# A chain of recurrent layers on one core: r, c and p products in two halves of 64 columns, and TensorE's loop over two steps

## Chip, cores and metric

The kernel runs on 1 core of one Trainium2 chip. The metric is the device time of one execution in microseconds. Times are given as in the trace; "4041.36" is a moment, in microseconds from the start of the profiled span.

## What is computed

Four layers follow each other on x of shape 2 x 2048 x 512 (batch B = 2, T = 2048 time steps, D = 512), each added to its input. `cond` is 2 x 512. All is fp32.

```python
x = x + rnn(x, cond)        # h = tanh(h @ Wh + x_t @ Wx + b), step by step
x = x + x * softmax(q . x / sqrt(D), over the 2 batch rows)
x = x + tanh(x @ W_ih.T + (cond @ W_hh.T + b_hh + b_ih))
x = x + gru(x, cond)

# gru, step by step:
z = sigmoid([x_t, h] @ Wz + bz);  r = sigmoid([x_t, h] @ Wr + br)
c = tanh([x_t, r * h] @ Wh + bh)
h_new = (1 - z) * h + z * c                     # the output of the step
h = tanh(h_new @ Wp + bp) if (t + 1) % 4 == 0 and t < T - 1 else h_new
```

Both recurrences go through all 2048 steps in order. Within a step of the gru, c needs r, and the next step's r and z need c. The step after every fourth one needs the propagation p as well.

## The kernel before

The time axis is cut into 128 chunks (CHUNKS) of 16 steps (STEPS); 16 steps x 2 batch rows are the 32 rows (ROWS) of one quadrant. The 512 features lie as 128 partitions x 4 tiles (KT). The layers run as a pipeline over iterations i = 0 to 129: in iteration i the rnn does chunk i, the middle layers do chunk i - 1, and the gru does chunk i - 2 (LAG = 2). What of x does not depend on the recurrence is projected for a whole chunk at a time (`project_rnn_input`, `project_mid`, `project_gates`), goes through DRAM and comes back as "seeds": ScalarE copies the row of a step into a PSUM bank (L659), and TensorE adds the product with the state to it.

TensorE runs one list of products. A step's products are r, z, c, l in this order (`group`): r and z of the gru from the state, c from rh = r * h, and l, the rnn's step. Each of the four has the state (128 partitions x 2 columns) as its stationary operand and 128 columns of weights as its moving one. `seeded_product` (L398) issues 4 tiles k x 4 quadrants j of them:

```python
for k in range(KT):
    if ready is not None and k in (0, FRONT):
        pe.wait_ge(ready[k // FRONT], count)
    for j in range(NJ):
        last = nc.tensor.matmul(psum[QUAD * j:QUAD * j + B, 0:P], stationary(k), w[:, k, P * j:P * (j + 1)], ...)
```

The chip runs an fp32 matmul in two passes, so the trace shows x32 for a product of 16 matmuls. The four quadrants j write to four groups of partitions.

After r's product VectorE transposes the bank in two pieces (L539), k = 0 (32 columns, "front") and k = 1 to 3 (96 columns, "others"); ScalarE takes tanh of each piece (L714); VectorE makes rh of each piece (L602); TensorE's c product waits for the front piece at k = 0 and for the others at k = 1. From c to the new state it is the same: transposes of the pieces (L539), tanh (L724), the scan (L647) that writes `h_ring`, and TensorE's next r. TensorE has other work meanwhile: z between r and c, l between c and the next r. After the fourth step of a group (PROP = 4) stand the product p, and one projection of the middle layers: the input of the third layer (`project_mid`) in group q = 0, halves of the gates' input (`project_gates`, 384 columns) in q = 1 and 2, the rnn's input (`project_rnn_input`) in q = 3. Then r of the next group needs tanh of p (L734).

The softmax's logits (L434, 32 columns) come after step 2 of a chunk. GpSimd does the middle layers' elementwise work, and adds the gru's output to x3 once for four steps (`outputs`, L319).

TensorE's code is unrolled in iterations 0 to 2 and 126 to 129. Between them is a loop over i (L504), in it one over the four groups q (L505) whose body holds four steps (r, z, c, l four times), with branches that choose the logits (L507) and the projection (L511, L512, L517). Register and branch instructions are in the same queue as the matmuls. The q loop ends with adding to q, a compare-and-branch back, and one register instruction at its head (FUSED_REGOPS) that works out the counts of the step; at the end of i also the i loop's, two moves and a branch.

Of the kernel before, what the change touches and what calls it, by code (L numbers as in the profile page):

```python
# [34 lines left out]
B, T, D = 2, 2048, 512  # L35
P = 128
QUAD = 32
# [5 lines left out]
PROP = 4  # L43
# [3 lines left out]
FRONT = 1  # L47


def cond_resid_kernel(nc, xT, condT, w_rnn_x, w_rnn_h, b_rnn, w_ih, w_hh, b_ih, b_hh,  # L50
# [5 lines left out]
    with ctx:  # L56
# [6 lines left out]
        def piece_sems(name):  # L63
            return [sem(name + "_front"), sem(name + "_others")]
# [53 lines left out]
        l_ring = sb("l_ring", PROP, KT, B)  # L118
# [4 lines left out]
        h_prop = sb("h_prop", KT, B)  # L123
# [4 lines left out]
        h_ring = sb("h_ring", PROP, KT, B, 2)  # L128

        def bank(name):  # L130
            return ctx.enter_context(nc.psum_tensor(name, [P, 512], fp32))
        ps_r, ps_z, ps_c, ps_l, ps_p, ps_logit, ps_mid, ps_proj = (
            bank(n) for n in ("ps_r", "ps_z", "ps_c", "ps_l", "ps_p", "ps_logit", "ps_mid", "ps_proj"))
# [4 lines left out]

        r_T, c_T, p_T = ([bank[:, P:2 * P].rearrange("p (k r) -> p k r", k=KT)[:, k, :] for bank, k in
                          ((front, slice(0, FRONT)), (others, slice(FRONT, KT)))]  # L140
                         for front, others in ((ps_p, ps_r), (ps_p, ps_c), (ps_r, ps_p)))
# [10 lines left out]
        r_seeded, r_product = sem("r_seeded"), sem("r_product")  # L152
        r_T_done, r_tanh_done = piece_sems("r_T_done"), piece_sems("r_tanh_done")
        z_seeded, z_product, z_T_done, z_tanh_done = (sem(n) for n in ("z_seeded", "z_product", "z_T_done", "z_tanh_done"))
        c_seeded, c_product = sem("c_seeded"), sem("c_product")
        c_T_done, c_tanh_done = piece_sems("c_T_done"), piece_sems("c_tanh_done")
        h_neg_half_done, z_done, kept_done = sem("h_neg_half_done"), sem("z_done"), sem("kept_done")
        rh_ready, h_ready = piece_sems("rh_ready"), piece_sems("h_ready")

        p_seeded, p_product = sem("p_seeded"), sem("p_product")  # L160
        p_T_done, p_ready = piece_sems("p_T_done"), piece_sems("p_ready")
# [32 lines left out]

        def rnn_behind(i, u):

            return not isinstance(i, int) or 0 < STEPS * i + u <= STEPS * CHUNKS
# [4 lines left out]

        def first_step(i, u):

            return isinstance(i, int) and i == LAG and u == 0
# [10 lines left out]

        PIECES = [(slice(0, FRONT), slice(0, QUAD * FRONT)), (slice(FRONT, KT), slice(QUAD * FRONT, P))]

# [3 lines left out]
        def _(sp):  # L222
# [43 lines left out]
            def iteration(i):  # L266
# [22 lines left out]
                if gru:  # L289
                    sp.wait_ge(y_ready, GROUPS * (i - LAG + 1))  # L290
                    sp.dma_start(out[i - LAG, :, :, :], y[:, :, :]).then_inc(stored, 16)
# [5 lines left out]
        def _(pool):  # L297
# [16 lines left out]
            def outputs(i, q):  # L314

                pool.wait_ge(h_ready[1], STEPS * (i - LAG) + PROP * (q + 1))
                rows = slice(PROP * B * q, PROP * B * (q + 1))
                for k in range(KT):
                    last = tt(y[:, k, rows].rearrange("p (t b) -> p t b", b=B), x3[:, k, rows].rearrange("p (t b) -> p t b", b=B),  # L319
                              h_ring[:, :, k, :, 1], ALU.add)  # L320
                last.then_inc(y_ready, 1)

            def iteration(i):
                rnn, mid, gru, proj = running(i)
                if mid:
# [15 lines left out]

                    pool.wait_ge(top_done, i)
# [5 lines left out]
                    tt(denom[:, :], epair[:, :, 0], epair[:, :, 1], ALU.add).then_inc(denom_done, 1)  # L348
                    pool.wait_ge(inv_done, i)
# [6 lines left out]
                if gru:  # L356
                    after(pool, stored, 16 * (i - LAG))
                    outputs(i, 0)
                if mid:
# [5 lines left out]
                    last.then_inc(mid_pre_done, 1)  # L365
                    pool.wait_ge(mid_tanh_done, i)
                    tt(x3_new[:, :, :], x2[:, :, :], mid_tanh[:, :, :], ALU.add).then_inc(x3_new_done, 1)
                if gru:
                    for q in range(1, GROUPS):
                        outputs(i, q)  # L370
                    pool.wait_ge(y_ready, GROUPS * (i - LAG + 1))
# [7 lines left out]
        def _(pe):  # L379
# [9 lines left out]
            def seeded_product(psum, stationary, w, ready, count):  # L389
# [4 lines left out]
                for k in range(KT):  # L394
                    if ready is not None and k in (0, FRONT):
                        pe.wait_ge(ready[k // FRONT], count)
# [3 lines left out]
                return last  # L400

# [19 lines left out]
            for psum in (ps_l, ps_z, ps_p, ps_r, ps_c):  # L421
                open_bank(psum).then_inc(banks_open, 1)
# [3 lines left out]
            pe.wait_ge(states_set, 2)  # L426
# [4 lines left out]
            def softmax_logits(i):  # L431
                pe.wait_ge(qx_sum_done, i)
                for j in range(NJ):
                    last = nc.tensor.matmul(ps_logit[QUAD * j:QUAD * (j + 1), 0:ROWS], ones[:, :], qx_sum[:, :], start=True, stop=True)  # L434
# [13 lines left out]
            def group(i, t_rnn, t_gru, q, logits, projection):  # L448

                rnn, mid, gru, proj = running(i)
                for u in range(PROP):
                    if gru:
                        if u == 0:
                            ready, count = (p_ready, t_gru) if not first_step(i, PROP * q) else (None, None)
                            state = lambda k: h_prop[:, k, :]
                        else:
                            ready, count = h_ready, t_gru + u
                            state = lambda k: h_ring[:, u - 1, k, :, 1]  # L460
                        if first_step(i, PROP * q + u):
                            pe.wait_ge(r_seeded, 1)
                            pe.wait_ge(c_seeded, 1)
                            pe.wait_ge(p_seeded, PROP)
# [323 lines left out]
```

## Time and profile before

| | |
|---|---|
| median of 3 runs | 8794.18 us |
| range of the runs | 8787.57 to 33782.32 us |
| the profiled execution | 8793.52 us |
| its span | 8791.7 us |
| granted TensorE clock | 0.997 of full |
| busy: TensorE, VectorE, ScalarE, GpSimd | 8661.0, 5044.1, 4687.6, 997.6 us |
| the chain that ended last | TensorE 98%, issue 1% |

A row of the timeline merges instructions of one kind that follow each other. Its length reaches to the modelled end of the last matmul, and consecutive rows of TensorE overlap by that, so the pace is read from the starts. "PEld" is the load of the stationary operand, and a bracket says how long the engine sat idle and what released it. "PEldq" rows are instructions that only TensorE's queue handles: branches and registers. "issue" is waiting that no semaphore explains.

### The profile page before, as it was taken

How to read it: one execution, taken by the hardware profiler on the slowest of the kernel's cores; microseconds unless marked ns; L12 is line 12 of the kernel's file. 1: busy time of each engine (PE TensorE's matmuls, PEld its weight loads, DVE VectorE, ACT ScalarE, POOL GpSimd, SP SyncE). 2: the span in 40 equal slices, each digit the busy share in tenths (PEclk: the TensorE clock that was granted, in tenths of full speed). 3: DMA queues.
4: the chain of work that ended last, by engine and by line, in shares of the span. 5: the costliest groups of instructions: out<-in, count | busy, mean ns of one | idle time of the engine just before them, and what ended most of it. 6: DMA issues, size and time to landing. Idle time of an engine off the chain costs nothing.

```text
span 8791.7 us, 669547 instructions
## 1 busy us (share of the span) xinstructions
PE 8661.0 (99%) x291880; PEld 6952.4 (79%) x291880; DVE 5044.1 (57%) x26506; ACT 4687.6 (53%) x26367; POOL 997.6 (11%) x4362
## 2 busy tenths in 40 slices
PE   8999999999999999999999999999999999999998
PEld 6778777877787778778787778777877787778776
DVE  3555555555555555555555555555555555555555
ACT  3555555555555555555555555555555555555554
POOL 1111111111111111111111111111111111111110
PEclk8999999999999999999999999999999999999999
DMA  1000000000000000000000000000000000000000
GB/s 67 11 12 10 10 11 12 10 10 10 13 10 10 10 13 10 10 10 12 11 10 10 11 12 10 10 11 12 10 10 10 13 10 10 10 13 10 10 11 11
DMA packets 133369, 105.97 MB, mean 12 GB/s; under 512 B 14976, under 2 KB 132096, under 8 KB 132096
## 3 DMA queue, kind: packets, MB, share of 16 engines
q1 hardware_dynamic: 133248, 104.20, 3.9%
q8 instruction: 95, 1.56, 0.1%
q14 instruction: 26, 0.21, 0.0%
HBM read 62.20 MB, written 41.94 MB: 12 GB/s over the span
## 4 chain that ended last, share of the span: by engine, by line
PE 98%; issue 1%; DVE 0%; ACT 0%; DMA 0%; SPq 0%; POOL 0%; DVEq 0%; ACTq 0%
PE ps_r L398 23%; PE ps_c L398 22%; PE ps_l L398 21%; PE ps_z L398 20%; PE ps_p L398 6%; PE ps_mid L385 5%; PE ps_proj L385 2%; DVE l_T L536 0%; DVE ps_p L539 0%; PE ps_logit L434 0%; DMA rnn_h<-w_rnn_h 0%; DVE h_ring L647 0%; ACT l_ring L685 0%; ACT ps_l L659 0%; ACT scan_add L724 0%
## 5 line engine op out<-in xcount | busy, mean ns | idle before, releaser
L398 PE MATMUL ps_l<-rnn_h,l_ring 128*2 128x128 f32 x65536 | 2179.3, 274 | 26.8 <-ACT ps_l L659 26.8
L398 PE MATMUL ps_c<-c_h,rh 128*2 128x128 f32 x65536 | 2165.0, 272 | 6.3 <-DVE rh L602 2.4
L398 PEld LDWEIGHTS ps_c<-c_h,rh 128*2 128x2 f32 x65536 | 1397.2, 84 | 543.8 <-DVE rh L602 376.3
L398 PEld LDWEIGHTS ps_l<-rnn_h,l_ring 128*2 128x2 f32 x65536 | 1723.8, 85 | 112.2 <-ACT ps_l L659 36.9
L398 PE MATMUL ps_r<-r_h,h_ring 128*2 128x128 f32 x49152 | 1671.7, 272 | 18.7 <-DVE h_ring L647 18.7
L398 PE MATMUL ps_z<-z_h,h_ring 128*2 128x128 f32 x49152 | 1623.8, 273 | 0.2 <-issue 0.2
L398 PEld LDWEIGHTS ps_r<-r_h,h_ring 128*2 128x2 f32 x49152 | 994.9, 83 | 542.4 <-DVE h_ring L647 478.9
L398 PEld LDWEIGHTS ps_z<-z_h,h_ring 128*2 128x2 f32 x49152 | 1291.6, 85 | 50.4 <-issue 0.6
L539 DVE STREAM_TRANSPOSE ps_p<-ps_r 128x32 f32<-128x32 f32 x2048 | 473.4, 231 | 1329.0 <-PE ps_r L398 1329.0
L539 DVE STREAM_TRANSPOSE ps_p<-ps_c 128x32 f32<-128x32 f32 x2048 | 473.6, 231 | 1128.3 <-PE ps_c L398 1128.3
L319 POOL TENSOR_TENSOR y<-x,h_ring 128x8 f32<-128x8 f32 x2048 | 347.6, 201 | 4951.9 <-DVE h_ring L647 4951.9
L718 ACT ACTIVATE z_tanh<-z_T 128x8 f32<-128x8 f32 x2048 | 428.6, 209 | 883.1 <-DVE z_T L536 883.0
L647 DVE TENSOR_TENSOR_SCAN h_ring<-scan_mul,scan_add 128x4 f32<-128x4 f32 (+1 forms) x4096 | 720.8, 178 | 160.6 <-ACT scan_add L724 0.4
L685 ACT ACTIVATE l_ring<-l_T 128x8 f32<-128x8 f32 x2048 | 429.4, 210 | 703.7 <-DVE l_T L536 703.7
L724 ACT ACTIVATE scan_add<-ps_p 128x2 f32<-128x2 f32 x2048 | 352.4, 172 | 838.3 <-DVE ps_p L539 838.3
L714 ACT ACTIVATE r_tanh<-ps_p 128x2 f32<-128x2 f32 x2048 | 352.5, 172 | 817.1 <-DVE ps_p L539 812.7
L602 DVE SCALAR_TENSOR_TENSOR rh<-r_tanh,h_neg_half 128x2 f32<-128x2 f32 (+1 forms) x4096 | 683.8, 169 | 165.2 <-ACT r_tanh L714 0.7
L536 DVE STREAM_TRANSPOSE z_T<-ps_z 128x128 f32<-128x128 f32 x2048 | 648.7, 317 | 131.4 <-PE ps_z L398 1.6
L536 DVE STREAM_TRANSPOSE l_T<-ps_l 128x128 f32<-128x128 f32 x2048 | 648.4, 317 | 67.9 <-PE ps_l L398 65.7
L398 PE MATMUL ps_r<-r_h,h_prop 128*2 128x128 f32 x16384 | 541.0, 272 | 58.6 <-issue 53.2
L398 PEld LDWEIGHTS ps_r<-r_h,h_prop 128*2 128x2 f32 x16384 | 406.1, 84 | 239.8 <-issue 140.8
L539 DVE STREAM_TRANSPOSE ps_c<-ps_c 128x96 f32<-128x96 f32 x2048 | 595.0, 291 | 0.0
(85 smaller groups left out, 9399.0 us busy)
## 6 DMA issues: line engine op xcount, KB each, us to landing
gates_spill<-gates_rows SPq DMA_DIRECT2D x128, 192.0 KB, 1.9
gates_seeds<-gates_spill SPq DMA_DIRECT2D x512, 48.0 KB
x_next<-xT SPq DMA_DIRECT2D x128, 64.0 KB, 1.7
x_mid<-xT SPq DMA_DIRECT2D x128, 64.0 KB, 1.7
rnn_spill<-rnn_rows SPq DMA_DIRECT2D x128, 64.0 KB, 1.5
rnn_seeds<-rnn_spill SPq DMA_DIRECT2D x512, 16.0 KB
y_out<-y SPq DMA_DIRECT2D x128, 64.0 KB, 1.6
rcz_x<-w_rc_x SPq DMA_DIRECT2D x1, 2048.0 KB, 9.0
```

Of the source, the lines that this page charges most:

```text
L319: last = tt(y[:, k, rows].rearrange("p (t b) -> p t b", b=B), x3[:, k, rows].rearrange("p (t b) -> p t b", b=B), h_ring[:, :, k, :, 1], AL ...
L385: last = nc.tensor.matmul(psum[QUAD * j:QUAD * j + rows, 0:width], stationary(k), weights(k, j), start=(k == 0), stop=(k == KT - 1))
L398: last = nc.tensor.matmul(psum[QUAD * j:QUAD * j + B, 0:P], stationary(k), w[:, k, P * j:P * (j + 1)], start=False, stop=(k == KT - 1), sk ...
L536: return nc.vector.transpose(tile, psum[:, 0:P])
L539: nc.vector.transpose(pieces[n].rearrange("p k r -> p (k r)"), psum[:, PIECES[n][1]]).then_inc(T_done[n], inc)
L602: nc.vector.scalar_tensor_tensor(rh[:, k, :], r_tanh[:, k, :], 1.0, h_neg_half[:, k, :], ALU.subtract, ALU.mult).then_inc(rh_ready[n], 1)
L647: nc.vector.tensor_tensor_scan(h_ring[:, u % PROP, k, :, :].rearrange("p k b s -> p (k b s)"), scan_mul[:, k, :, :].rearrange("p k b s -> ...
L685: nc.scalar.activation(l_ring[:, u % PROP, :, :], l_T[:, :, 0:B], ACT.Tanh).then_inc(l_ready, 1)
L714: nc.scalar.activation(r_tanh[:, k, :], r_T[n][:, :, 0:B], ACT.Tanh, scale=-0.5).then_inc(r_tanh_done[n], 1)
L718: nc.scalar.activation(z_tanh[:, :, :], z_T[:, :, 0:B], ACT.Tanh, scale=0.5).then_inc(z_tanh_done, 1)
L724: nc.scalar.activation(scan_add[:, k, :, 0], c_T[n][:, :, 0:B], ACT.Tanh).then_inc(c_tanh_done[n], 1)
```

## The change

- r and c are computed in two halves of 64 columns (n = 0, 1; W = 64). Half n of all quadrants goes to a bank of its own: `ps_r` and `ps_c` are now two banks each. p shares the banks of c at other columns, and the logits share the bank of `ps_proj`. The order of the 8 parts (k, n), each of 4 matmuls, is: (0,0), (0,1), (1,0) once the low piece of the state is there, then, after the wait for the high piece, the rest of n = 0, a semaphore increment, the rest of n = 1, another. For p the early parts are (0,0) and (1,0).
- The pieces of transposes, tanh, rh and scan are now k = 0, 1 ("low") and k = 2, 3 ("high"), 64 columns each.
- TensorE's unrolled iterations 2 and 126 to 129 become loops: i from 2 to 127, in it q over four groups, in it v over two pairs of steps; and the same for 128 and 129 without l.
- The state lies in `h_even`, `h_odd` and `h_pre` (the step ahead of a propagation) in place of a ring of four. GpSimd adds the output after each step, between its other work; before a scan VectorE waits until GpSimd has done the step before last.
- ScalarE seeds the two banks with one instruction of 128 elements; at a group's last step the seed of c comes after the tanh of p.

```diff
-            def seeded_product(psum, stationary, w, ready, count):
+            def seeded_product(psum, stationary, w):
...
+            def halved_product(pair, at, stationary, w, ready, count, done, inc, early=((0, 0), (0, 1), (1, 0))):
...
+                def part(k, n):
+                    for j in range(NJ):
+                        last = nc.tensor.matmul(pair[QUAD * j:QUAD * j + B, n, at:at + W], stationary(k), w[:, k, P * j + W * n:P * j + W * (n + 1)],
+                                                start=False, stop=(k == KT - 1), skip_group_check=True)
+                    return last
+
+                if ready is not None:
+                    pe.wait_ge(ready[0], count)
+                for k, n in early:
+                    part(k, n)
+                if ready is not None:
+                    pe.wait_ge(ready[1], count)
+                for n in range(2):
+                    for k in range(KT):
+                        if (k, n) not in early:
+                            last = part(k, n)
+                    last.then_inc(done[n], inc)
...
-            with nc.Fori(LAG + 1, CHUNKS - 2, engines=[pe.engine]) as i:
-                with nc.Fori(0, GROUPS, engines=[pe.engine], head_slot={pe.engine: 0}) as q:
...
+            with nc.Fori(LAG, CHUNKS, engines=[pe.engine], head_slot={pe.engine: 0}) as i:
+                with nc.Fori(0, GROUPS, engines=[pe.engine]) as q:
+                    with nc.Fori(0, PROP // 2, engines=[pe.engine]) as v:
+                        t = STEPS * i + PROP * q + 2 * v
+                        for u in range(2):
+                            step(True, True, t + u, t + u - STEPS * LAG, u)
+                        with pe.If(v < 1):
                             with pe.If(q < 1):
-                                project_mid(i)
+                                softmax_logits(i)
                             with pe.Else():
-                                project_gates(i, (0, 1))
+                                pe.nop()
                         with pe.Else():
...
+                            propagation(STEPS * i + PROP * q + PROP - 1 - STEPS * LAG)
...
-            def transpose_piece(n, pieces, psum, T_done, inc=1):
-                nc.vector.transpose(pieces[n].rearrange("p k r -> p (k r)"), psum[:, PIECES[n][1]]).then_inc(T_done[n], inc)
+            def transpose_piece(n, product, pair, at, pieces, T_done, count, inc=1):
+                dve.wait_ge(product[n], count)
+                nc.vector.transpose(pieces[n].rearrange("p k r -> p (k r)"), pair[:, n, at:at + W]).then_inc(T_done[n], inc)
...
-                                if u % PROP == 0:
-
-                                    after(dve, y_ready, GROUPS * (i - LAG) + u // PROP)
+                                after(dve, y_ready, t - 1)
...
+            def output(i, u):
+
+                t = STEPS * (i - LAG) + u
+                h, ready, count, _ = scanned(t, u)
+                pool.wait_ge(ready[1], count)
+                rows = slice(B * u, B * (u + 1))
+                tt(y[:, :, rows], x3[:, :, rows], h[:, :, :, 1], ALU.add).then_inc(y_ready, 1)
```

How TensorE's instructions stand in the loop, first before: the end of a group's second step (the l product, then the branch around the logits) and the start of its third.

```order
L398 MATMUL ps_l<-rnn_h,l_ring 2x128 x16
L507 COMPARE_AND_BRANCH
L434 MATMUL ps_logit<-qx_sum,ones 32x32 x4
L507 UNCONDITIONAL_BRANCH
L398 MATMUL ps_r<-r_h,h_ring 2x128 x16
L466 REGISTER_ALU
```

And in the changed kernel, from the l product of a pair's first step to the end of the pair.

```order
L420 MATMUL ps_l<-rnn_h,l_ring 2x128 x16
L431 MATMUL ps_r<-r_h,h_even 2x64 x32
L420 MATMUL ps_z<-z_h,h_even 2x128 x16
L431 MATMUL ps_c<-c_h,rh 2x64 x32
L420 MATMUL ps_l<-rnn_h,l_ring 2x128 x16
L542 COMPARE_AND_BRANCH
L543 COMPARE_AND_BRANCH
L479 MATMUL ps_proj<-qx_sum,ones 32x32 x4
L543 UNCONDITIONAL_BRANCH
L545 UNCONDITIONAL_BRANCH
```

Between the second and the third step there stood one branch. Now the pair ends there: a branch on v, one on q, one to the loop's end (after the logits, or in their absence), and the rows that follow below.

The end of the loop body in the changed kernel, from the projection of group 3 on (L538 is the loop over v, L537 over q, L536 over i).

```order
L558 UNCONDITIONAL_BRANCH
L560 UNCONDITIONAL_BRANCH
L538 REGISTER_ALU
L538 COMPARE_AND_BRANCH
L537 REGISTER_ALU
L537 COMPARE_AND_BRANCH
L536 REGISTER_ALU
L536 COMPARE_AND_BRANCH
```

The same place before, where L505 is the loop over q and L504 the one over i.

```order
L385 MATMUL ps_proj<-rnn_x,x_next 32x128 x16
L519 UNCONDITIONAL_BRANCH
L505 REGISTER_ALU
L505 COMPARE_AND_BRANCH
L504 REGISTER_ALU
L504 COMPARE_AND_BRANCH
```

The added loop's register addition and its branch stand at the end of every pair. Behind the branch back comes the register instruction at the loop's head (L538 ISA) before the next r. Where q or i goes on, two moves set v anew, and two more set q.

VectorE between two states, before: from the transposes of r to the halved state.

```order
L539 STREAM_TRANSPOSE ps_p<-ps_r 128x32 [waits r_product]
L539 STREAM_TRANSPOSE ps_r<-ps_r 128x96
L602 SCALAR_TENSOR_TENSOR rh<-r_tanh,h_neg_half 128x2 [waits h_neg_half_done,r_tanh_done_front]
L602 SCALAR_TENSOR_TENSOR rh<-r_tanh,h_neg_half 128x6 [waits r_tanh_done_others]
L536 STREAM_TRANSPOSE z_T<-ps_z 128x128 [waits z_product]
L539 STREAM_TRANSPOSE ps_p<-ps_c 128x32 [waits c_product]
L637 SCALAR_TENSOR_TENSOR scan_add<-z_tanh,h_neg_half 128x8 [waits z_tanh_done]
L539 STREAM_TRANSPOSE ps_c<-ps_c 128x96
L647 SCALAR_TENSOR_TENSOR h_ring<-scan_mul,scan_add 128x4 [waits kept_done,z_done,c_tanh_done_front]
L647 SCALAR_TENSOR_TENSOR h_ring<-scan_mul,scan_add 128x12 [waits c_tanh_done_others]
```

The same stretch in the changed kernel.

```order
L605 STREAM_TRANSPOSE ps_r<-ps_r 128x64 [waits r_product_low]
L605 STREAM_TRANSPOSE ps_r<-ps_r 128x64 [waits r_product_high]
L659 SCALAR_TENSOR_TENSOR rh<-r_tanh,h_neg_half 128x4 [waits h_neg_half_done,r_tanh_done_low]
L659 SCALAR_TENSOR_TENSOR rh<-r_tanh,h_neg_half 128x4 [waits r_tanh_done_high]
L601 STREAM_TRANSPOSE z_T<-ps_z 128x128 [waits z_product]
L605 STREAM_TRANSPOSE ps_c<-ps_c 128x64 [waits c_product_low]
L693 SCALAR_TENSOR_TENSOR scan_add<-z_tanh,h_neg_half 128x8 [waits z_tanh_done]
L605 STREAM_TRANSPOSE ps_c<-ps_c 128x64 [waits c_product_high]
L702 SCALAR_TENSOR_TENSOR h_even<-scan_mul,scan_add 128x8 [waits kept_done,z_done,y_ready,c_tanh_done_low]
L702 SCALAR_TENSOR_TENSOR h_even<-scan_mul,scan_add 128x8 [waits c_tanh_done_high]
```

The instructions are the same in number and order. The transposes wait for a half of the product each, and the scan also for GpSimd's addition.

## Rows read from the trace of the kernel before

**Rows 1.** The page: span, and TensorE's part of the busy times.
```profile
span 8791.7 us, 669547 instructions
...
PE 8661.0 (99%) x291880; PEld 6952.4 (79%) x291880; DVE 5044.1 (57%) x26506; ACT 4687.6 (53%) x26367; POOL 997.6 (11%) x4362
```
**Rows 2.** Timeline of TensorE's matmuls, 4020 to 4080: start, us, engine, line, operation, tiles.
```profile
4022.84 1.47 PE L385 MATMUL ps_mid<-rcz_x,x_new 128*32 128x384 f32 x16
4024.13 1.06 PE L398 MATMUL ps_r<-r_h,h_prop 128*2 128x128 f32 x32
...
4038.80 1.10 PE L398 MATMUL ps_p<-prop_w,h_ring 128*2 128x128 f32 x32
4039.89 1.08 PE L385 MATMUL ps_proj<-rnn_x,x_next 128*32 128x128 f32 x32
4041.36 1.05 PE L398 MATMUL ps_r<-r_h,h_prop 128*2 128x128 f32 x32 [0.39 <-issue]
...
4046.91 1.05 PE L398 MATMUL ps_c<-c_h,rh 128*2 128x128 f32 x32
4047.78 1.06 PE L398 MATMUL ps_l<-rnn_h,l_ring 128*2 128x128 f32 x32
4048.65 0.24 PE L434 MATMUL ps_logit<-qx_sum,ones 128*32 128x32 f32 x8
4048.72 1.10 PE L398 MATMUL ps_r<-r_h,h_ring 128*2 128x128 f32 x32
...
4057.02 1.06 PE L385 MATMUL ps_mid<-ih,x 128*32 128x128 f32 x32
4058.09 1.05 PE L398 MATMUL ps_r<-r_h,h_prop 128*2 128x128 f32 x32
```
**Rows 3.** Timeline of all engines, 4000 to 4020: from one c product to the next.
```profile
4003.24 1.05 PE L398 MATMUL ps_c<-c_h,rh 128*2 128x128 f32 x32
...
4004.36 0.23 DVE L539 STREAM_TRANSPOSE ps_p<-ps_c 128x32 f32<-128x32 f32 x1 [0.62 <-PE ps_c L398]
...
4004.55 0.29 DVE L539 STREAM_TRANSPOSE ps_c<-ps_c 128x96 f32<-128x96 f32 x1
4004.63 0.17 ACT L724 ACTIVATE scan_add<-ps_p 128x2 f32<-128x2 f32 x1 [0.40 <-DVE ps_p L539]
4004.83 0.43 DVE L647 TENSOR_TENSOR_SCAN h_ring<-scan_mul,scan_add 128x4 f32<-128x4 f32 x2
...
4005.05 0.11 PEld L398 LDWEIGHTS ps_p<-prop_w,h_ring 128*2 128x2 f32 x8 [0.18 <-DVE h_ring L647]
...
4005.32 0.55 PEld L398 LDWEIGHTS ps_p<-prop_w,h_ring 128*2 128x2 f32 x24 [0.16 <-DVE h_ring L647]
```
**Rows 4.** TensorE's queue by line, short stretches: xcount, ns min/median/max, first and last start.
```profile
L507 PEldq COMPARE_BRANCH  x1: 77/77/77, 4048.0 to 4048.0; - x1
...
L507 PEldq COMPARE_BRANCH  x1: 210/210/210, 4064.7 to 4064.7; - x1
...
L505 PEldq COMPARE_BRANCH  x2: 76/122/169, 4040.3 to 4040.9; - x2
L505 PEldq ALU_OP  x1: 32/32/32, 4040.2 to 4040.2; - x1
L505 PEldq MOVE  x1: 29/29/29, 4040.9 to 4040.9; - x1
L505 PEldq FUSED_REGOPS  x1: 133/133/133, 4041.2 to 4041.2; - x1
...
L504 PEldq ALU_OP  x1: 36/36/36, 4040.4 to 4040.4; - x1
L504 PEldq COMPARE_BRANCH  x1: 208/208/208, 4040.5 to 4040.5; - x1
L504 PEldq MOVE  x1: 38/38/38, 4040.8 to 4040.8; - x1
```
**Rows 5.** Timeline of TensorE's matmuls, 4108.5 to 4114: the next iteration's first product.
```profile
4109.25 1.06 PE L398 MATMUL ps_r<-r_h,h_prop 128*2 128x128 f32 x32 [0.40 <-issue]
```

More of the change, by code:

```diff
@@ L312, in _, with outputs @@
             pool.wait_ge(h_term_ready, 1)
[L314 to L321, printed above, removed]
+            def output(i, u):
[4 more added lines that the diff above has]
+                tt(y[:, :, rows], x3[:, :, rows], h[:, :, :, 1], ALU.add).then_inc(y_ready, 1)
+            def outputs(i, gru, steps):
+                if gru:
+                    for u in steps:
+                        output(i, u)
             def iteration(i):
@@ L340, in iteration @@
                     tt(qx_sum[:, :], qx_half[:, 0, :], qx_half[:, 1, :], ALU.add).then_inc(qx_sum_done, 1)
+                if gru:
+                    after(pool, stored, 16 * (i - LAG))
+                outputs(i, gru, range(0, 2))
+                if mid:
                     pool.wait_ge(top_done, i)
@@ L497, in unrolled, with propagation, projections @@
+            def propagation(t_gru):
+                halved_product(ps_c, P_AT, lambda k: h_pre[:, k, :, 1], prop_w, h_pre_ready, t_gru + 1, p_product, PROP,
+                               early=((0, 0), (1, 0)))
+            def projections(i, q):
+                if q == 0:
+                    project_mid(i)
+                if q in (1, 2):
+                    project_gates(i, ((0, 1), (2, 3))[q - 1])
+            for i in range(LAG):
                 if i == 1:
                     pe.wait_ge(loaded_gru, 16 * 8)
-                for q in range(GROUPS):
-                    group(i, STEPS * i + PROP * q, STEPS * (i - LAG) + PROP * q, q, lambda: logits(q), lambda: projection(q))
@@ L502, in _ @@
-            for i in range(LAG + 1):
-                unrolled(i)
-            with nc.Fori(LAG + 1, CHUNKS - 2, engines=[pe.engine]) as i:
-                with nc.Fori(0, GROUPS, engines=[pe.engine], head_slot={pe.engine: 0}) as q:
-                    def logits():
-                        with pe.If(q < 1):
-                            softmax_logits(i)
-                    def projection():
-                        with pe.If(q < 2):
+                for u in range(STEPS):
+                    step(True, False, STEPS * i + u, None, u)
+                    if i > 0 and u == 1:
+                        softmax_logits(i)
+                    if u % PROP == PROP - 1:
+                        if i > 0:
+                            projections(i, u // PROP)
+                        if u // PROP == 3:
+                            project_rnn_input(i + 2)
@@ L522, in _ @@
-                    group(i, STEPS * i + PROP * q, STEPS * (i - LAG) + PROP * q, q, logits, projection)
-            for i in range(CHUNKS - 2, CHUNKS + LAG):
-                unrolled(i)
+                            propagation(STEPS * i + PROP * q + PROP - 1 - STEPS * LAG)
+                            with pe.If(q < 2):
+                                with pe.If(q < 1):
+                                    projections(i, 0)
+                                with pe.Else():
+                                    projections(i, 1)
```

239 lines of the change are left out of this document (126 added, 113 removed).

## The prediction

> **What bounds the kernel now.** I read the page first: TensorE is busy for 8661.0 of 8791.7 us [rows 1]. Since matmuls overlap, that does not say how much of it is idle, so I went to the timeline of its matmuls and read starts against starts [rows 2]. A product of 128 columns takes 0.87 us when nothing holds it up: c at 4046.91, l at 4047.78, the logits at 4048.65. It is 8 sets of four matmuls (one per quadrant, side by side), so 0.109 us a set. The gates' projection, 4 sets of 384 columns, takes 4022.84 to 4024.13 = 1.29 us. An iteration of 16 steps runs from 4041.36 [rows 2] to 4109.25 [rows 5] = 67.89 us. What TensorE has to do in it is 64 products r, z, c, l and 4 of p at 0.872 = 59.3, and mid 0.87, gates 2 x 1.29, rnn input 0.89, logits 0.07 = 4.4: 63.7 us. So 4.2 us per iteration are gaps.
>
> The next question is what the gaps are. The timeline of all engines shows the way from one c to the next product [rows 3]: c starts at 4003.24, its transposes at 4004.36 and 4004.55, the tanh at 4004.63, the scan at 4004.83, and the waiting product loads at 4005.05 for the front piece and at 4005.32 for the others. That is 1.81 us from c's start. c and l together fill 1.744, the first k another 0.22 against 0.27 needed. So about 0.11 us are lost here, and about 0.07 from r to c, where the way is alike: near 0.19 a step, 3.2 us per iteration. The other 1.0 us is at group ends, where TensorE's queue works through branches: r stands at 4041.36 with 0.39 "issue", 1.47 us after the projection's start at 4039.89, where 0.89 is work [rows 2].
>
> **Part 1, the halves: what they free.** The first half of c is complete after five of eight parts instead of after all. With parts of 0.111 us (below), the last matmul of half 0 starts about 0.52 us after c's start, against 0.78 for the whole product before. Behind that last start the old chain needed 4005.05 - 4004.02 = 1.03 us; so the low piece is there at about 1.55, the high one 0.34 later at 1.89. TensorE is with c and l until 1.76, and three early parts carry it to 2.10. Both pieces have 0.2 us of room. The transposes are 64 columns where 32 and 96 took 0.23 and 0.29 [rows 3], so their sum is no greater. The waits for h and rh, 3.2 us per iteration, go. Late next is TensorE itself: its columns, and its branches.
>
> **Part 2, what the halves cost.** There are 36 halved products per iteration (16 r, 16 c, 4 p), each now 16 sets of 64 columns. No row has that shape. The nearest are 128 columns (0.109 a set), 384 (1.29 / 4 = 0.3225) and the logits, 2 sets of 32 columns in 4048.65 to 4048.72 = 0.035 a set [rows 2]. The slope from 128 to 384 is 0.00083 per column, which gives 0.0556 at 64; the line from 32 to 128 gives 0.060. I take 0.0556: the logits also load 32 stationary columns, which these don't. A product is then 0.890 instead of 0.872: 36 x 0.018 = +0.65 us per iteration. The bounds: at 0.0545, half of a set before, nothing; at 0.060, +3.2.
>
> The logits' row also speaks against a limit by the number of instructions: 8 matmuls in 0.07 us are 9 ns each [rows 2], and the new ones need to be issued every 14 ns.
>
> **Part 3, the branches.** They cost nothing while matmuls stand in the queue. How long is that cover? The branch behind l is taken up at 4048.0 [rows 4], when l, begun at 4047.78, still has until 4048.65: 0.64 us, about 24 matmuls of 128 columns. And what does an instruction of the queue take? From 4040.2 to 4041.2 stand seven of them, with 0.032, 0.076, 0.036, 0.208, 0.038, 0.029 and 0.169 us = 0.588 [rows 4]. So about 0.06 us lie behind each. A branch not taken costs 0.14, one taken 0.27, an unconditional one 0.23, an addition 0.10, a move 0.095, and the register instruction at the loop's head, until the load behind it, 0.185 (4041.175 within rounding, to 4041.36). Which branch is which: L507 took 77 ns where the logits follow, 210 where they are jumped over [rows 4]. The group end with mid tests these prices: what follows it is 0.23 + 0.10 + 0.27 + 0.185 = 0.79 against a cover of 0.64, so r should be 0.15 late. It starts 1.07 after mid, where 0.87 is work: 0.20 late [rows 2].
>
> Now the changed loop, by the order of its instructions.
> Between the pairs of a group (4 times per iteration): 0.14 (v) + 0.27 (q) + 0.23 + 0.10 + 0.27 + 0.185 = 1.195. The cover behind l is 0.64. So 0.56 us stand open where before one branch of 0.27 was hidden: 3 x 0.56. In group 0, with the logits, 1.12 - 0.64 - 0.07 = 0.41. Together 2.1 us.
> After p: its cover is 24 matmuls of 64 columns now, 0.33. Before mid 0.33 is needed, before the gates 0.46, before the rnn's input 0.27 + 0.27 + 0.14 + 0.20 = 0.88: open are 0, 0.13, 0.13, 0.55 = 0.8 us.
> After the projection: 0.23 + 0.10 + 0.14 + 0.10 + 0.27 + 2 x 0.095 + 0.185 = 1.215. After mid 0.58 of it is open; after the gates nothing, since all 16 of their matmuls fit in the queue and last 1.29. At the end of i it is 0.43 more, 1.65 - 0.64 = 1.0. Together 1.6 us.
> The sum is 4.5 us per iteration, against 1.0 before.
>
> **Part 4, the rest.** VectorE has the same instructions, with a wait for GpSimd in front of the scan. GpSimd adds one step's output (0.2 us) right after its scan, and VectorE asks for it two steps later, some 7 us; between two of the adds stands at most one piece of the middle layers. Hidden, at no cost; from below it can't gain, and from above I allow 2 us per iteration. ScalarE's seed of c moves behind p's tanh, with r and z, 1.76 us, still ahead of the c that needs it. In iterations 128 and 129 there is no l, so the chain binds: about 0.3 us less in one step of two, less the longer loop ends. With that and fewer first passes over unrolled code I take -5 us, between -12 and +5.
>
> **The sum.** One iteration: 63.7 + 0.65 + 4.5 = 68.84 us against 67.89: +0.95. Over the 126 iterations of the loop that is +120 us, and -5 for the ends. The sum is made against the profiled execution, 8793.5 us, which agrees with the median of 8794.2: 8908 us, 1.3% above.
>
> **The rivals.**
> *The branches stay hidden, and it is faster.* If the queue's work ran beside the matmuls also between the pairs and at the loop ends, 4.5 would shrink to about the old 1.0, and an iteration would take 65.4 us: -2.5 x 126 = -315, 8475 us. It decides from the point where the cover is 1.2 us instead of 0.64. For it speaks that the gaps of 3.2 us do go; against it that the old group ends already show the queue's time in full.
> *The second piece is late.* If the high pieces still come after the early parts, by half of the old wait, 1.6 us per iteration stay: +200, 9110 us. The room of 0.2 us speaks against it, and that the transposes of the halves now wait in VectorE's order behind those of z and l.
> *GpSimd holds the scan.* If the adds queue behind x2 or behind the wait for mid's transpose, a step can stall for 1 us twice per iteration: +250, 9160 us. The place would be steps 4 to 7 of a chunk.
> *Matmuls have a floor.* If a set of 64 columns took as long as one of 128, a halved product would be 1.74 us: 36 x 0.87 x 128 = +4000, some 12900 us. The logits' 9 ns per matmul speak against it; for it, that they are only 8 in a row.
> The Trainium skill ("TensorE: Matmul & The Clock Gate", section "Wait — 56ns, not 53.3ns?") states that start to start never drops below about 25 ns however few the columns are, which would make a halved product 64 x 25 = 1.6 us by the page, an estimate, and a total near this rival's. The logits' rows do not agree with it for matmuls in four quadrants.
>
> **How the numbers follow.** About 2% is what a measurement of this kernel tells from no change, so 8618 and 8970 are the borders. My forecast's case has 0.70; its own range is 8820 to 9010, from the set at 0.0545 to 0.0575 and the branch prices within 15%, and about 0.12 of it lies above 8970. Hidden branches have 0.08, the late piece 0.10, GpSimd 0.08, the floor 0.04. Of the hidden branches all is faster by over 2%: 0.08. Above 8970 lie 0.12 and most of the last three, 0.19: 0.31. The rest, 0.61, is within 2%. The range takes in part of the late piece and of GpSimd's: 8780 to 9090.
>
> **What would show it.** r, c and p with 64 matmuls in about 0.89 us, start to next start; no wait of r and c for the scan and rh worth naming; between the second and third step of each group a gap of 0.5 to 0.6 us marked "issue"; an iteration of 68.8 us. Wrong would be: issue gaps under 0.3 us between the pairs (the first rival), waits of r for the scan of over 1 us per iteration (the second), waits of the scan for GpSimd (the third), halved products over 1 us (the fourth).

## The result and the profile after

The changed kernel takes 9020.7 us (median, 9011.8 to 9024.6) where the kernel before takes 8794.2 beside it (8787.6 to 8807.9; a fourth run of it, of 33782.3 us in a slow state, is left out): a ratio of 1.0253, 95% interval 1.0233 to 1.0274, so it is slower. The forecast was 8908 us. The time lies in the forecast's range, but the loss is 2.5% where 1.3% was said.

The page of the changed kernel; [rows 1] stands against its first lines:

```profile
span 9010.0 us, 973858 instructions
PE 8520.0 (95%) x439312; PEld 7912.4 (88%) x439312; DVE 5349.5 (59%) x26507; ACT 4701.2 (52%) x26367; POOL 1070.1 (12%) x4362
...
q8 instruction: 19, 0.31, 0.0%
...
PE 94%; issue 5%; DVE 0%; ACT 0%; DMA 0%; SPq 0%; DVEq 0%; ACTq 0%; POOL 0%
```

"issue" has gone from 1% to 5% of the chain, and no data wait has come in its place. The largest waits of the weight loads, 1000 to 8000 us, first of the kernel before, then of the changed one (waited for, us in total, times, longest):

```profile
PEld ps_r L398 <- DVE h_ring L647: 370.9, 1952, 0.3
PEld ps_c L398 <- DVE rh L602: 300.7, 1650, 0.3
PEld ps_p L398 <- DVE h_ring L647: 131.6, 722, 0.3
PEld ps_r L398 <- issue: 112.9, 309, 0.7
```
```profile
PEld ps_r L431 <- issue: 516.8, 806, 1.1
PEld ps_mid L409 <- issue: 126.3, 603, 0.4
```

The waits for the state and for rh are gone. What r waits for now is its own queue. 806 waits in 7000 us are 8 per iteration of 69.44 us: the start of each pair of steps.

The timeline of TensorE's matmuls, changed kernel, as [rows 2] of the one before (start, us, engine, line, operation):

```profile
4020.23 1.07 PE L431 MATMUL ps_r<-r_h,h_odd 128*2 128x64 f32 x64 [0.39 <-issue]
...
4023.76 1.08 PE L431 MATMUL ps_r<-r_h,h_even 128*2 128x64 f32 x64
4024.65 1.06 PE L420 MATMUL ps_z<-z_h,h_even 128*2 128x128 f32 x32
4025.53 1.08 PE L431 MATMUL ps_c<-c_h,rh 128*2 128x64 f32 x64
4026.42 1.06 PE L420 MATMUL ps_l<-rnn_h,l_ring 128*2 128x128 f32 x32
4027.86 1.08 PE L431 MATMUL ps_r<-r_h,h_odd 128*2 128x64 f32 x64 [0.38 <-issue]
...
4034.93 1.08 PE L431 MATMUL ps_c<-prop_w,h_pre 128*2 128x64 f32 x64
4035.99 1.50 PE L409 MATMUL ps_mid<-rcz_x,x_new 128*32 128x384 f32 x16
4037.30 1.08 PE L431 MATMUL ps_r<-r_h,h_odd 128*2 128x64 f32 x64
...
4069.24 1.08 PE L431 MATMUL ps_c<-prop_w,h_pre 128*2 128x64 f32 x64
4070.76 1.08 PE L409 MATMUL ps_proj<-rnn_x,x_next 128*32 128x128 f32 x32 [0.44 <-issue]
4072.65 1.07 PE L431 MATMUL ps_r<-r_h,h_odd 128*2 128x64 f32 x64 [0.80 <-issue]
...
4089.67 1.07 PE L431 MATMUL ps_r<-r_h,h_odd 128*2 128x64 f32 x64 [0.39 <-issue]
```

Read start to start: a halved product takes 4024.65 - 4023.76 = 0.89 us, a whole one 0.87. Between the pairs l is followed by r after 1.44 us (4026.42 to 4027.86), of which 0.57 is a gap. The bracket shows only 0.38 of it, since the modelled ends reach into the gap. Behind p, the gates' projection starts 1.06 us after p where 0.89 is work, and the rnn's projection 1.52 us after it, 0.63 late. Added up over one iteration (4020.23 to 4089.67 = 69.44 us), the gaps are 2.2 us between pairs, 1.1 behind p and 1.65 behind the projections: 4.96 us, where the kernel before had 4.2 of waits and branches together. On the mean of 100 iterations, from the start of one logits product to that of the hundredth after it, the changed kernel takes 69.51 us (744.17 to 7695.06) and the kernel before 67.87 (723.34 to 7509.93).

### The profile page after: what moved, and what is told of

Its sections match the earlier page's. It is cut to its first block, busy times and chain, and to the rows that moved or that the text cites. A ratio compares the mean times of both kernels' runs of the same rounds, so it can differ in the third digit from the quotient of the medians.

```text
span 9010.0 us, 973858 instructions
## 1 busy us (share of the span) xinstructions
PE 8520.0 (95%) x439312; PEld 7912.4 (88%) x439312; DVE 5349.5 (59%) x26507; ACT 4701.2 (52%) x26367; POOL 1070.1 (12%) x4362
## 4 chain that ended last, share of the span: by engine, by line
PE 94%; issue 5%; DVE 0%; ACT 0%; DMA 0%; SPq 0%; DVEq 0%; ACTq 0%; POOL 0%
PE ps_c L431 25%; PE ps_r L431 22%; PE ps_l L420 20%; PE ps_z L420 20%; PE ps_mid L409 6%; PE ps_proj L409 2%; DVE ps_c L605 0%; DVE l_T L601 0%; PE ps_proj L479 0%; DMA rnn_h<-w_rnn_h 0%; ACT scan_add L785 0%; ACT l_ring L746 0%; ACT ps_l L714 0%; DMA gates_seeds<-gates_spill 0%; DVE h_even L702 0%
## 5 line engine op out<-in xcount | busy, mean ns | idle before, releaser
L431 PE MATMUL ps_c<-c_h,rh 128*2 128x64 f32 x131072 | 2209.9, 219 | 0.2 <-issue 0.2
L605 DVE STREAM_TRANSPOSE ps_r<-ps_r 128x64 f32<-128x64 f32 x4096 | 1087.0, 265 | 1444.9 <-PE ps_r L431 1289.0
L605 DVE STREAM_TRANSPOSE ps_c<-ps_c 128x64 f32<-128x64 f32 x5118 | 1358.1, 265 | 790.4 <-PE ps_c L431 732.0
L420 PEld LDWEIGHTS ps_l<-rnn_h,l_ring 128*2 128x2 f32 x65536 | 1644.9, 85 | 78.9 <-ACT ps_l L714 36.9
L431 PEld LDWEIGHTS ps_r<-r_h,h_odd 128*2 128x2 f32 x65536 | 920.3, 85 | 674.8 <-issue 666.3
L431 PE MATMUL ps_r<-r_h,h_odd 128*2 128x64 f32 x65536 | 1102.3, 219 | 358.8 <-issue 351.9
L431 PE MATMUL ps_r<-r_h,h_even 128*2 128x64 f32 x65536 | 1104.3, 219 | 11.1 <-DVE h_even L702 9.5
L420 PE MATMUL ps_z<-z_h,h_odd 128*2 128x128 f32 x32768 | 1085.3, 273 | 0.0
L420 PE MATMUL ps_z<-z_h,h_even 128*2 128x128 f32 x32768 | 1084.1, 273 | 0.9 <-issue 0.9
L431 PEld LDWEIGHTS ps_r<-r_h,h_even 128*2 128x2 f32 x65536 | 1012.2, 85 | 24.8 <-DVE h_even L702 12.8
L420 PEld LDWEIGHTS ps_z<-z_h,h_odd 128*2 128x2 f32 x32768 | 821.7, 85 | 16.5
```

Of the source, the lines that this page charges most:

```text
L431: last = nc.tensor.matmul(pair[QUAD * j:QUAD * j + B, n, at:at + W], stationary(k), w[:, k, P * j + W * n:P * j + W * (n + 1)], start=Fals ...
L605: nc.vector.transpose(pieces[n].rearrange("p k r -> p (k r)"), pair[:, n, at:at + W]).then_inc(T_done[n], inc)
```

## The experiments

Each was run against the kernel before on the same chip; "the change" is the changed kernel. Only e4 and e2 start from the kernel before, all others from the change.

**e2: one more branch where it should be hidden; e3: the same where it should be open.** An addition and a taken branch more, behind l of the second step (e2, kernel before), and behind each pair of steps (e3, the change, there with `LAG + 1`):

```diff
+                        with pe.If(i + q < LAG + 2):
+                            pe.wait_ge(ones_set, 1)
                         with pe.If(q < 1):
                             softmax_logits(i)
```

> The kernel before, with a register addition and a branch that is taken, put behind the l product of each group's second step (0.37 us of the queue's time, 4 times per iteration). If work of the queue costs nothing while matmuls stand in it (0.63 us behind l), the sum of 0.37 and the old branch's 0.27 is covered, and the time stays at 8795 us within 15. If each branch costs its own time, it is 1.5 x 123 = 180 us more, 8980.

> The changed kernel with the same register addition and taken branch ahead of the branch on v, so at the end of both pairs of a group. At the end of the first pair nothing covers it: 4 x 0.37 = 1.5 us per iteration. At the end of the second 0.42 of the old work and 0.37 stand against a cover of 0.63: 4 x 0.16 = 0.6. Together 2.1 x 126 = +265 us, 9285 us. If the gap between pairs came from something else than the queue's instructions (a wait, or the jump back itself), the time would stay near 9020.

Measured: e2 8799.9 against 8800.5 us, ratio 0.9997 (0.9987 to 1.0006). It costs nothing. e3 9254.5 us, ratio 1.0517 (1.0500 to 1.0535), 234 us above the change. The timeline of e3 between two pairs:

```profile
4057.39 1.06 PE L420 MATMUL ps_l<-rnn_h,l_ring 128*2 128x128 f32 x32
4059.20 1.02 PE L431 MATMUL ps_r<-r_h,h_odd 128*2 128x64 f32 x60 [0.75 <-issue]
```

From l to r are 1.81 us here, 1.44 in the change: the 0.37 us of the two instructions are paid in full. Behind the second pair p starts only 0.14 us late, since there is still cover under l. An iteration is 1.9 us longer where 2.1 were expected. The same instructions cost nothing or everything by where they stand. That holds for the theory that the queue runs 0.64 us ahead of a whole product's end and no more.

**e1: four steps in the loop, written out.** The loop over v is gone, nothing else changes; the body of the q loop is 1901 instructions of TensorE's compiled program, where the kernel before has some 1300:

```diff
-                    with nc.Fori(0, PROP // 2, engines=[pe.engine]) as v:
-                        t = STEPS * i + PROP * q + 2 * v
-                        for u in range(2):
-                            step(True, True, t + u, t + u - STEPS * LAG, u)
...
+                    t = STEPS * i + PROP * q
+                    for u in range(PROP):
+                        step(True, True, t + u, t + u - STEPS * LAG, u)
...
```

> The changed kernel with the loop over pairs of steps written out: the body of the loop over q holds four steps, with halves as they are, and the branch on the logits stands alone after the second step. If the time lost is the branches at the end of each pair (2.2 us per iteration in the trace of the changed kernel) and at the group ends (0.4 us less at the end of groups 0 and 3 each), an iteration takes 66.4 us instead of 69.4, and the kernel 8640 us, 1.7% below the kernel before. If the halves themselves, or the waits on GpSimd, were what costs, it would stay above 8950. If a body of some 1900 instructions does not stay in the queue's memory, each turn waits for code, several us per group, and it is over 10000 us.

Measured: 15959.5 us, ratio 1.8128. The last of the three cases held. The line of e1's page on the queue that brings instructions (packets, MB), and its timeline around a group's end:

```profile
q8 instruction: 4549, 74.53, 2.2%
```
```profile
8051.99 1.49 PE L409 MATMUL ps_mid<-rcz_x,x_new 128*32 128x384 f32 x14 [1.37 <-issue]
8057.84 1.08 PE L431 MATMUL ps_r<-r_h,h_odd 128*2 128x64 f32 x64 [4.36 <-issue]
8058.73 1.90 PE L420 MATMUL ps_z<-z_h,h_odd 128*2 128x128 f32 x32
```

These are 74.5 MB in 4549 packets, so 16 KB each, where the change has 19 packets. Over the 504 rounds of the q loop in 126 iterations that is 9 packets a round. The body's code is loaded anew every round, in 9 blocks, and TensorE waits for it, 4.36 us at the loop's head. Behind such a stop the clock is lower too: the z product at 8058.73 takes 1.66 us to the next start (8060.39), the granted clock from 8060 to 8064 us is 0.73, and the run's mean is 0.89 of full. So with both products in halves four steps don't fit, and the short loop is the price of the halves. The Trainium skill ("Runtime: NRT & Kernel Launch", section "Instruction fetch mechanics") states that TensorE's instruction memory holds 2048 instructions and is filled in blocks of 256. The size of the packets fits that, at 64 bytes an instruction. That a body under 2048 is loaded anew does not follow from it.

**e7 and e8: the same with fewer instructions.** At 256 instructions a block, e1's body lies in 8 blocks, and the ninth packet would be the block fetched ahead. e7 has r whole (128 columns in one bank), c and p in halves, four steps: 1645 instructions, 7 blocks. e8 has r and c in halves, p whole, and the rnn's projection moved behind the q loop: 7 blocks in the q loop, 8 in the whole iteration.

```diff
 e7:
-                    halved_product(ps_r, R_AT, lambda k: h[:, k, :, 1], r_h, ready, count, r_product, 1)
+                    whole_product(ps_r, 0, R_AT, lambda k: h[:, k, :, 1], r_h, ready, count, r_product, 1)
 e8:
-                halved_product(ps_c, P_AT, lambda k: h_pre[:, k, :, 1], prop_w, h_pre_ready, t_gru + 1, p_product, PROP,
+                whole_product(ps_c, 0, P_AT, lambda k: h_pre[:, k, :, 1], prop_w, h_pre_ready, t_gru + 1, p_product, PROP,
...
+                with pe.If(i < CHUNKS - 2):
+                    project_rnn_input(i + 2)
```

> e6_r_whole with the loop of four steps: its body is 1645 instructions of TensorE, 7 blocks of 256, against 1901 in 8 blocks for e1_four_steps. Theory (e1 was slow because its 8 blocks and the one fetched ahead, 9 packets a group, did not fit; 7 and one ahead do): no packets of instructions per group, 63.7 of work, 0.4 for 20 seams, 1.7 for rh, 1.0 for the branches at a group's end: 66.8 us an iteration, 8663 us, with the ends 8680 (8620 to 8740), faster than both kernels. Rival (what decides is a smaller memory, or any body above the 1300 instructions of the kernel before): fetched again each group, above 12000 us.

> The change with four steps in the loop, r and c in halves, p whole, and the projection of the next chunk's RNN input moved out of the loop over groups to the end of the iteration: the loop over groups is 1765 instructions, 7 blocks of 256, the whole iteration 1848, 8 blocks. Theory (8 blocks hold and the next one is fetched ahead): one round of fetches in each iteration instead of four, about 14 us as in a group of e1_four_steps (31.2 against 17.4): 8520 + 125 x 14 = 10270 us. Rival (blocks are kept by use, an eighth block costs nothing): 63.7 of work, 0.6 for 32 seams, 1.0 to 1.2 for branches, no waits: 65.5 us an iteration, 8520 us, faster than both kernels. A third (the memory is smaller than 7 blocks): above 12000 us.

Measured: e7 8818.4 us, ratio 1.0020 (1.0010 to 1.0030); e8 10075.1 us, ratio 1.1450. The pages' lines on q8, of e7 and then of e8, and e8's timeline at an iteration's end:

```profile
q8 instruction: 21, 0.34, 0.0%
```
```profile
q8 instruction: 1147, 18.79, 0.9%
```
```profile
4077.33 1.08 PE L409 MATMUL ps_proj<-rnn_x,x_next 128*32 128x128 f32 x32 [0.45 <-issue]
4083.53 1.88 PE L431 MATMUL ps_r<-r_h,h_odd 128*2 128x64 f32 x64 [5.12 <-issue]
```

The limit behaved as the theory says: 10270 us was expected for e8. Seven blocks stay (21 packets in the whole run). With eight in the iteration there are 1147 packets, 9 per iteration, and one round of waiting per iteration, which brings it to some 78 us. So a loop stays in place here up to 7 blocks; the eighth sets off a reload of all. That it goes by whole blocks is inferred: the runs show loops of 1645 and, in e9, 1781 instructions that stay, and of 1848 and 1901 that don't, and nothing between. e7 missed its number, though: 8680 was expected, and it is no faster than the kernel before. Its steps take the 3.61 us expected, but its group ends cost about 1 us more per iteration than the 1.0 I had put in. The next experiment shows most of why: p is in halves in it.

**e10: p alone whole, in the loop of two steps.** The edit is e8's on p.

> The change with p alone as a whole product of 128 columns. Theory (a halved product at the end hides 0.23 us of branches, a whole one 0.64, so that only 0.4 of the 1.13 us behind p stays, as in e5_whole_two_steps; and four seams of 0.018 go): -0.8 us an iteration, 9020 - 100 = 8920 us (8900 to 8940). Rival (the branches are one chain: what p hides turns up behind the projection or at r's wait): 9010 to 9020 us.

Measured: 8880.5 us, ratio 1.0089 (1.0071 to 1.0107), 140 us below the change. First the queue behind p in the change, its first branch and the loop's head (line, operation, count, ns, first and last start), from a group that takes the gates' projection:

```profile
L549 PEldq COMPARE_BRANCH  x1: 77/77/77, 4035.6 to 4035.6; - x1
...
L538 PEldq FUSED_REGOPS  x1: 160/160/160, 4037.1 to 4037.1; - x1
```

then the same place in e10:

```profile
L558 PEldq COMPARE_BRANCH  x1: 208/208/208, 4062.6 to 4062.6; - x1
```
```profile
4062.37 1.06 PE L452 MATMUL ps_c<-prop_w,h_pre 128*2 128x128 f32 x32
4063.24 1.48 PE L409 MATMUL ps_mid<-rcz_x,x_new 128*32 128x384 f32 x16
```

In the change p starts at 4034.93 and would end at 4035.82; the queue comes to its first branch at 4035.6, some 0.2 us before. In e10 p starts at 4062.37 and ends at 4063.24, and the queue comes to its first branch at 4062.6: 0.6 us before. So a halved product at the end of a run of matmuls hides about 0.2 us of branches, a whole one 0.6, as l does. The branch on v that the queue takes ahead of p is in both kernels. It is not needed for the short cover either: in e7, which has none there, p starts at 4029.34 and the queue is at its first branch at 4030.0, again 0.2 us before p's end. The projection follows p at once, 0.87 us later, where the change has 1.06. Of the 1.13 us behind p about 0.2 stay (before the rnn's projection), and the mean iteration takes 68.46 us instead of 69.51: 1.05 x 126 = 132 of the 140 us. More came back than my 0.8, and 8880.5 lies below my 8900 to 8940, since I had left 0.4 us in place. The halves of p save no wait that TensorE would feel: r starts 1.45, 1.29, 1.29 and 1.93 us after the four projections in e10, and 1.47, 1.31, 1.32 and 1.89 in the change. They are more than half of the change's whole loss.

**e4, e5, e6: the parts of the change apart.** e4 is the kernel before with equal pieces (`FRONT = 2`), so with products of 128 columns and the long loop. e5 is the change with r, c and p whole: equal pieces and the short loop. e6 is the change with r alone whole. The edits are those of e7 and e8, on c too for e5.

> The kernel before with pieces of 64 and 64 columns instead of 32 and 96 for transposes, tanh, rh and scan, and whole products of 128 columns. If what removes the waits is that the first half of a product is complete early, equal pieces alone do nothing: the second wait of r (0.04 us) goes, the first gets 0.03 longer; 8795 us within 40. If the sizes of the pieces are what helps, it would lose the old waits of 3.2 us per iteration, and be 200 to 400 us faster.

> The change with r, c and p as whole products of 128 columns again (pieces of two and two k tiles), everything else as in the change: the loop of two steps alone. Theory (the loop costs its open branches, the halves gave back the waits): per iteration 63.7 us of work, 2.2 between pairs, 1.1 behind p and 1.65 behind the projection as measured in the change, and the waits of e4_equal_pieces again, 1.7 for rh (16 x 0.11) and 0.9 for the scan inside the pairs: 71.2 against 69.44, so 9020 + 126 x 1.8 = 9245 us (9200 to 9290). Rival (the loop is nearly free, the halved products are what costs): as e4_equal_pieces, 8875 us.

> The change with r alone as a whole product, c and p in halves, loop of two steps. Theory: c waits for rh again, 16 x 0.11 = 1.7 us, and 16 seams of 0.018 = 0.3 go: +1.4 us an iteration, 9020 + 126 x 1.4 = 9197 us (9150 to 9240). Rival (r's halves were worth nothing, since z's 0.87 us cover rh): 9020 - 36 = 8984 us.

Measured: e4 8874.7 us, ratio 1.0084 (1.0067 to 1.0101); e5 9267.2 us, ratio 1.0532 (1.0515 to 1.0550); e6 9169.2 us, ratio 1.0422 (1.0405 to 1.0440). One step of e4, and two of e5 across a pair's end:

```profile
4039.84 1.06 PE L398 MATMUL ps_l<-rnn_h,l_ring 128*2 128x128 f32 x32
4040.82 1.05 PE L398 MATMUL ps_r<-r_h,h_ring 128*2 128x128 f32 x32
4041.70 1.06 PE L398 MATMUL ps_z<-z_h,h_ring 128*2 128x128 f32 x32
4042.67 1.06 PE L398 MATMUL ps_c<-c_h,rh 128*2 128x128 f32 x32
```
```profile
4063.57 1.06 PE L420 MATMUL ps_l<-rnn_h,l_ring 128*2 128x128 f32 x32
4064.61 1.05 PE L452 MATMUL ps_r<-r_h,h_even 128*2 128x128 f32 x32
...
4084.92 1.06 PE L420 MATMUL ps_l<-rnn_h,l_ring 128*2 128x128 f32 x32
4086.41 1.05 PE L452 MATMUL ps_r<-r_h,h_odd 128*2 128x128 f32 x32 [0.43 <-issue]
```

In e4 l to r takes 0.98 and z to c 0.97 where 0.87 is work: 0.1 us of wait at each, somewhat more than the 0.19 a step of [rows 3]. The uneven pieces of the kernel before were worth 74 us. A reason may be that a smaller first piece is through the chain sooner, so that TensorE starts earlier; no run separates this. I had expected no difference. e5 puts the short loop on top and pays 393 us more: 1.49 us from l to r between pairs, and a wait of 0.17 inside them. e5 also holds the change's other edits (GpSimd's addition after each step, the state in other tiles), which no run takes alone. 9245 was expected, so the open branches with their measured prices explain all but some 20 us. Halving c and p takes 98 us off (e6, 9169 of the 9197 expected), and halving r another 149 (the change): steps of 3.53 instead of 3.61 us. The halves of r and c do what they are for: with p left whole (e10 against e5) they take 387 us off. Without them the short loop would have cost 5.3%.

**e9: what the two findings give together.** Four steps in both of TensorE's loops; r and c in halves, but r whole at the first step of each group and p whole; the rnn's projection at the end of the iteration as in e8. The whole iteration is 1781 instructions, 7 blocks.

```diff
-                    halved_product(ps_r, R_AT, lambda k: h[:, k, :, 1], r_h, ready, count, r_product, 1)
+                    if u == 0:
+                        whole_product(ps_r, 0, R0_AT, lambda k: h[:, k, :, 1], r_h, ready, count, r_product, 1)
+                    else:
+                        halved_product(ps_r, R_AT, lambda k: h[:, k, :, 1], r_h, ready, count, r_product, 1)
...
-                    with nc.Fori(0, PROP // 2, engines=[pe.engine]) as v:
...
+                    t = STEPS * i + PROP * q
+                    for u in range(PROP):
+                        step(True, True, t + u, t + u - STEPS * LAG, u)
```

> Four steps in both loops; r and c in halves except r at the first step of each group of four, which is whole as p is; the projection of the next RNN input at the end of the iteration. The whole iteration is 1781 instructions of TensorE, 7 blocks of 256 (e8_p_whole_four: 1848, 8 blocks, one round of fetches per iteration). Theory (7 blocks stay, so no packets of instructions per iteration; no branch lies open between pairs and no wait for h or rh): 16 x 3.53 + 4 x 0.08 = 56.8 for the steps, 2.17 twice, 2.0 and 3.1 at the ends of the groups, 0.15 for the logits: 66.4 us an iteration; 126 of them and the 255 us around them that e7_r_whole_four shows: 8620 us (8580 to 8660), faster than both kernels. Rival (the closing branch and the blocks ahead count too, the round of fetches stays): about 10070 us.

Measured: 8554.2 us, ratio 0.9720 (0.9703 to 0.9737): 2.8% below the kernel before and 5.2% below the change. Page and timeline:

```profile
span 8550.4 us, 904256 instructions
...
q8 instruction: 23, 0.38, 0.0%
...
PE 98%; issue 1%; DVE 0%; ACT 0%; DMA 0%; SPq 0%; DVEq 0%; ACTq 0%; POOL 0%
```
```profile
4068.11 1.08 PE L432 MATMUL ps_r<-r_h,h_even 128*2 128x64 f32 x64
...
4071.64 0.24 PE L489 MATMUL ps_proj<-qx_sum,ones 128*32 128x32 f32 x8
4071.70 1.08 PE L432 MATMUL ps_r<-r_h,h_odd 128*2 128x64 f32 x64
...
4078.77 1.06 PE L453 MATMUL ps_c<-prop_w,h_pre 128*2 128x128 f32 x32
4079.64 1.06 PE L410 MATMUL ps_mid<-ih,x 128*32 128x128 f32 x32
4080.66 1.05 PE L453 MATMUL ps_r<-r_h,h_odd 128*2 128x128 f32 x32
```
```profile
PEld ps_c L432 <- DVE rh L675: 121.2, 530, 0.4
```

A step with both products in halves is 3.53 us, pair ends among them (4068.11 to 4071.64). The first of a group, where r is whole, takes 3.61 (4080.66 to 4084.27) or some 0.1 more: there c waits for rh again, as the last line says (1000 to 8000 us, about 5 waits an iteration). p, mid and the next r follow with 0.15 us lost. "issue" is at 1% again. An iteration takes 65.95 us, by 0.45 less than I had added up, so the time lies below the 8580 to 8660 expected.

## Why the prediction was right or wrong

**What bounds, and part 1: right.** TensorE's chain stayed the bound, and the waits of r and c for h and rh are gone: no row of them is left among the weight loads. e5 and e6, where the products are whole again, bring them back.

**Part 2, the halves' columns: right.** 0.0556 us a set was taken, 0.0558 measured; a product 0.893 instead of 0.890. 36 of them make 0.1 us an iteration more than said. Of the floor there is nothing to be seen: 64 matmuls in 0.89 us are 14 ns each. The 25 ns of the Trainium skill's page on matmuls ("TensorE: Matmul & The Clock Gate", section "Wait — 56ns, not 53.3ns?") do not hold for matmuls in four quadrants.

**Part 3, the branches: right in kind, too small by 0.5 us an iteration.** Between pairs 2.1 was said and 2.2 measured; e3 priced the branch, 0.37 us, as foreseen. After the projections 1.6 against 1.65. "After p: its cover is 24 matmuls of 64 columns now, 0.33", 0.8 in all, is the step that failed: the cover is about 0.2, the gaps 1.13, 0.33 more than said, and e10 shows that they hang on p's shape. I took the cover as a number of matmuls, 24, and scaled it by their length; 0.23 us are only some 16 of them. Why it is fewer than behind a whole product no run shows. The register instruction at a loop's head also takes 0.160 us instead of the 0.133 of [rows 4]; it stands in each of the 8 turns of the v loop.

**Part 4, the rest.** VectorE never waited long enough for GpSimd to be named: the adds after each step cost nothing that shows. "I take -5 us" for the ends is the second step that failed. The spans differ by 218 us; the loop's 126 iterations are 1.64 us longer each on the mean, 207, and the other 11 lie in the first and last passes. The granted clock (PEclk) and TensorE's busy time in the first pass, windows of the changed kernel (window, us, busy, matmuls, PEclk, DMA share, GB/s):

```profile
112.00:116.00 4.00, 0.55 (x11) 0.81 0.02 4
116.00:120.00 4.00, 3.10 (x92) 0.50 0.02 4
```
```profile
L543 PEldq COMPARE_BRANCH  x2: 65/1864/3664, 112.4 to 112.6; - x2
...
116.89 1.89 PE L431 MATMUL ps_r<-r_h,h_odd 128*2 128x64 f32 x64 [4.09 <-issue]
```

The jump behind the logits (L543) takes 3.66 us the first time, TensorE idles for 4.09 us, and then runs at half its clock, 1.2 GHz, in the window after. The first chunk of the gru takes 78.9 us (69.7 before), which is most of the 11. The second loop begins in the same way, with a branch (L571) of 2.7 us. I had reckoned with fewer first passes, which is true (19 packets of instructions instead of 95), but straight code was loaded without a stop, and the branches' targets were not. The kernel before has such stops too, two of them, 2.45 us (L505 at 166.6) and 2.42 us (L512 at 185.2). That this is loading of code is read from the trace, where one packet of instructions moves during each of the two long branches of the changed kernel, and was not tested by a run of its own.

**The sum.** 0.95 an iteration was said, 1.64 measured: 0.69 x 126 = 87 us. Of this the branches are 0.46 and the halves' columns 0.10; the rest is rounding and that the mean iteration is 0.07 longer than the one read above. The ends are 16 more, and the changed kernel's median is 9 us above its profiled execution, from which these are read. That is the 113 us between 8908 and 9021. The mechanism was right, then, and terms of the sum were too small.

**The rivals.** Hidden branches: out, by the change's own gaps and by e3. A late second piece: out, no wait left. GpSimd: out. The floor: out by the halved product's 0.89 us.

## What to carry to other kernels

Work in TensorE's queue that is no matmul costs nothing or its full time, by how far the queue is ahead at that place. Look at the shape of the last product in front of a branch: a whole product of 128 columns hid 0.6 us here, one in halves 0.2. Count a loop's instructions in blocks before splitting products or unrolling: here 7 blocks of 256 stayed in place and an eighth made every round load all of them. And when a change carries two edits because one needs the other, test each with the other undone: the halves were worth about 250 us (those of r and c 387, with p's taking 140 of it back), and the loop that made room for them cost 390.

## What the runs showed of the hardware that was not expected

- TensorE's loop of 1901 instructions was loaded anew in each round, 9 packets of 16 KB; one of 1781 was not. Such a round was 12 to 14 us longer, and the granted clock was lower with the stops (0.89 on the mean in e1, 0.96 in e8).
- The first time a branch of a loop was taken it could last 2.7 and 3.7 us (L571 and L543 of the changed kernel); TensorE stood still, and half clock followed.
- Equal pieces instead of 32 and 96 columns cost 0.8% by themselves (e4), though the sum of the transposes is the same.
